# One core, convolution attention and a routed feed-forward block: constants loaded behind the first half tile of x, an inverse root in 7 operations for 9, and the weight centring in another order

## The reference, cut to what matters

```
x = x + conv_attention(ln_c(x))              # ln_c: over the 64 channels, eps 1e-6
t = tokens(x)                                # (8, 1024, 64)
t = t + ffn(ln_t(t))                         # ln_t: over the 64 channels, eps 1e-5

conv_attention(x):                           # 8 heads of 8 channels
  q, k, v = Wqkv @ x + bqkv;  q *= 8 ** -0.5
  attn = softmax(q @ k.T over n, axis=-1)    # 8 x 8 in each head
  return Wout @ (attn @ v) + bout

ffn(x):                                      # 8 experts, 2 of them for each image
  logits = mean(x over n) @ Wr + br
  w = softmax(logits); w = softmax(w * capacity_scale); top 2, softmax again
  y = sum over the two experts e of w_e * (gelu(x @ W1[e] + b1[e]) @ W2[e] + b2[e])
  return layer_norm(y + x) * gamma + beta    # eps 1e-5
```

## Time and profile before

| what | value |
|---|---|
| median of 3 runs | 119.23 us (118.2, 119.23, 119.26) |
| span of the profiled execution | 117.0 us |
| its own total | not listed; the three runs lie 1.2 to 2.3 us above the span |
| busy: TensorE, VectorE, ScalarE, GpSimd | 80%, 59%, 43%, 35% of the span |
| granted TensorE clock, mean | 0.956 |

### The profile page before, as it was taken

The page is one execution under the profiler, slowest core; times in us unless marked ns, Lnnn a source line. Parts: engine busy times, 40 slices in busy tenths (PEclk is TensorE's granted clock), DMA queues, the critical chain, the costliest instruction groups (busy, mean ns, idle before and its releaser), DMA issues.

```text
span 117.0 us, 2060 instructions
## 1 busy us (share of the span) xinstructions
PE 94.2 (80%) x626; PEld 46.6 (40%) x629; DVE 68.5 (59%) x276; ACT 50.1 (43%) x76; POOL 40.7 (35%) x93
## 2 busy tenths in 40 slices
PE   0059998989997999676599879999999998989300
PEld 0023497976763546344133223233342333234100
DVE  0299996723374188489869106835185273769850
ACT  0400504615325435407666592892983769050000
POOL 3000724900006000236801649940460550095190
PEclk9999999999999999999558999999999999999985
DMA  3999960000000000002583000560000030004124
GB/s 76 330 421 401 404 248 0 6 0 0 0 0 6 0 0 0 0 0 62 121 203 70 3 3 0 123 146 6 0 3 0 0 150 35 0 17 182 70 90 179
DMA packets 4314, 9.81 MB, mean 84 GB/s; under 512 B 592, under 2 KB 848, under 8 KB 4304
## 3 DMA queue, kind: packets, MB, share of 16 engines
q1 hardware_dynamic: 3728, 8.34, 21.6%
q10 hardware_dynamic: 576, 1.34, 3.2%
HBM read 5.49 MB, written 2.10 MB: 65 GB/s over the span
## 4 chain that ended last, share of the span: by engine, by line
PE 52%; DVE 18%; issue 8%; POOL 6%; DMA 5%; POOLq 5%; ACT 3%; ACTq 0%; DVEq 0%
PE pC L1080 10%; PE pC L886 6%; DMA cst<-consts_dram 5%; POOL XT L220 4%; PE pA L1053 4%; PE pM L956 4%; DVE UF L626 4%; PE pB L1053 4%; PE pS L827 3%; POOLq L437 3%; PE pA L837 3%; PE pM L891 2%; PE pB L949 2%; PE pC L973 2%; PE pS L891 2%
## 5 line engine op out<-in xcount | busy, mean ns | idle before, releaser
L1080 PE MATMUL pC<-H,w2g 128*64 128x512 f32 x64 | 15.8, 603 | 0.5 <-POOL w2g L452 0.5
L362 ACT ACTIVATE H<-pA,b1g 128x1024 f32<-128x1024 f32 x8 | 8.9, 1111 | 8.8 <-PE pA L1053 8.8
L535 DVE BATCH_NORM_STATS2 bst<-XT 128x6 f32<-128x64 f32 x64 | 9.4, 214 | 5.1 <-DMA XT<-x_tok_dram 5.1
L227 POOL TENSOR_TENSOR UT<-XT,rt 128x1024 f32<-128x1024 f32 x3 | 6.7, 2243 | 14.8 <-issue 10.9
L210 POOL CAST R<-r 128x16 bf16<-128x16 f32 (+1 forms) x5 | 1.0, 203 | 29.2 <-DVE r L525 29.2
L220 POOL TENSOR_TENSOR XT<-XT,T 128x512 f32<-128x512 f32 x7 | 9.2, 1334 | 4.0 <-DVE XT L788 4.0
L956 PE MATMUL pM<-cst 128*128 128x480 f32 x6 | 4.6, 904 | 7.2 <-DMA cst<-consts_dram 7.2
L753 DVE TENSOR_TENSOR c<-b2g 64x1 f32<-64x1 f32 x8 | 5.7, 716 | 5.9 <-POOL w2g L452 5.8
L966 PE MATMUL pB<-cstb 128*128 128x512 bf16 x27 | 8.8, 489 | 0.2 <-issue 0.2
L362 ACT ACTIVATE H<-pB,b1g 128x1024 f32<-128x1024 f32 x8 | 8.9, 1117 | 0.0
L419 POOL TENSOR_TENSOR LO<-UF,HI 128x1024 f16<-128x1024 f32 x4 | 8.4, 2128 | 1.2 <-ACT HI L308 1.2
(11 more groups left out here) (193 smaller groups left out, 177.1 us busy)
## 6 DMA issues: line engine op xcount, KB each, us to landing
X<-x_cha_dram SPq DMA_DIRECT2D x4, 512.0 KB, 11.3
out_dram<-XT SPq DMA_DIRECT2D x8, 256.0 KB, 2.0
XT<-x_tok_dram SPq DMA_DIRECT2D x3, 512.0 KB, 7.8
ST<-HI SPq DMA_DIRECT2D x8, 128.0 KB, 2.4
ST<-LO SPq DMA_DIRECT2D x8, 128.0 KB, 2.4
w_sb<-w_dram ACTq DMA_DIRECT2D x1, 512.0 KB, 8.1
cstb<-constb_dram ACTq DMA_DIRECT2D x1, 304.0 KB, 9.7
XT<-x_tok_dram ACTq DMA_DIRECT2D x1, 256.0 KB, 4.5
```

What stands on the lines that cost most here:

```text
L227: engine.tensor_tensor(UT[:, p, :, 1:P + 1].rearrange("p j (b c) -> p j b c", b=2), XT[:, p, :].rearrange("p (j b c) -> p j b c", b=2, c=C ...
L362: nc.scalar.activation(H[:, step % 2, b, :], h_ps[b][:, :], ACT.Gelu, bias=b1g[:, p % 2, b, k:k + 1], scale=1.0 / (S_U * S_W)).then_inc(s[ ...
L535: return nc.vector.bn_stats(bst[:, p // 2, i % (2 * G2), :], XT[:, p, g * C:(g + 1) * C])
L1080: last = mm(half(y_ps[:, cols], b), w2g[:, p % 2, b, k, :], H[:, step % 2, b, cols], start=False, stop=(k == TOP - 1))
```

## The change

It does five things. (1) ScalarE's queue waits for the first half tile of XT before it issues cst, w_sb and cstb. (2) TensorE centres the attention weights first, then W1, then experts 0 to 3 of W2, all ahead of gram(0); the third warm_up is gone and the wait for cstb moves to turn2. ScalarE copies in the same order. (3) Experts 4 to 7 of W2 are centred where the first keep_awake stood, in front of att_b1(1). (4) rsqrt has seven operations: the seed in one tensor_scalar (times -0.5, plus the magic number), and one polynomial of third degree in t = y*y*v in place of two refinements. (5) variance1 has four operations where it had five.

```diff
-RSQRT = (8 / 3) ** 2
+RSQRT = 13.314428630185905
+RS_A0, RS_A1, RS_A2, RS_A3 = -3.0727744284785232, 1.6324990948619877, 2.8033168883754556, 4.4108093219280375
...
             act.dma_start(XT[:, 0, HALF:N], x_tok[:, 0, HALF:N]).then_inc(s_xt[0], 16)
+            act.wait_ge(s_xt_first, 16)
             act.dma_start(cst[:, :], consts).then_inc(s_cst, 16)
...
-            act.wait_ge(s["w1p"], 1)
-            nc.scalar.mul(w1hl[:, :, 0, :], pC[:, :].rearrange("p (e f) -> p e f", e=E), S_W).then_inc(s["w1h"], 1)
-
             act.wait_ge(s["wcp"], 1)
...
             nc.scalar.copy(wvc[:, :], pS[:, 300:300 + C]).then_inc(s["wcv"], 1)
+            act.wait_ge(s["w1p"], 1)
+            nc.scalar.mul(w1hl[:, :, 0, :], pC[:, :].rearrange("p (e f) -> p e f", e=E), S_W).then_inc(s["w1h"], 1)
             evac_gram(0)
...
-                link(nc.vector.tensor_scalar(q, v.bitcast(U32), 1, None, ALU.logical_shift_right), between)
-                link(nc.vector.tensor_scalar(y.bitcast(U32), q, -1.0, float(0x5F3759DF), ALU.mult, ALU.add), between)
+                y, t, q = (nwt[:, i, 0:m] for i in range(3))
+                link(nc.vector.tensor_scalar(y.bitcast(U32), v.bitcast(U32), -0.5, float(0x5F3759DF), ALU.mult,
+                                             ALU.add), between)
                 link(nc.vector.tensor_tensor(t, y, y, ALU.mult), between)
                 link(nc.vector.tensor_tensor(t, t, v, ALU.mult), between)
-                link(nc.vector.scalar_tensor_tensor(out=t, in0=t, scalar=-10.0 / 3.0, in1=t, op0=ALU.add,
+                link(nc.vector.scalar_tensor_tensor(out=q, in0=t, scalar=RS_A0, in1=t, op0=ALU.add,
                                                     op1=ALU.mult), between)
-                link(nc.vector.scalar_tensor_tensor(out=y, in0=t, scalar=5.0, in1=y, op0=ALU.add, op1=ALU.mult), between)
-                link(nc.vector.scalar_tensor_tensor(out=t, in0=y, scalar=-0.5 * (3 / 8) ** 2, in1=y, op0=ALU.mult,
+                link(nc.vector.scalar_tensor_tensor(out=t, in0=q, scalar=RS_A2, in1=t, op0=ALU.add,
+                                                    op1=ALU.add), between)
+                link(nc.vector.scalar_tensor_tensor(out=t, in0=q, scalar=RS_A1, in1=t, op0=ALU.add,
                                                     op1=ALU.mult), between)
-                link(nc.vector.tensor_tensor(t, t, v, ALU.mult), between)
-                nc.vector.scalar_tensor_tensor(out=out, in0=t, scalar=1.5, in1=y, op0=ALU.add,
+                nc.vector.scalar_tensor_tensor(out=out, in0=t, scalar=RS_A3, in1=y, op0=ALU.add,
                                                op1=ALU.mult).then_inc(done, 1)
...
-                nc.vector.tensor_tensor(cmp1[:, g, 1, :], ve, vo, ALU.add)
+                nc.vector.scalar_tensor_tensor(out=cmp1[:, g, 1, :], in0=ve, scalar=C * EPS_C, in1=vo, op0=ALU.add,
+                                               op1=ALU.add)
...
             pe.wait_ge(s_cst, 16)
             warm_up(2)
 
-            pe.wait_ge(s_w12, 16)
-            for h in range(2):
-                last = mm(pC[:, h * HALF:(h + 1) * HALF], cf("cend", 0, C), w12_sb[0:C, h * HALF:(h + 1) * HALF],
-                          start=True, stop=True)
-            last.then_inc(s["w1p"], 1)
             pe.wait_ge(s_wsm, 16)
...
             last.then_inc(s["wcp"], 1)
-            warm_up(1)
+            pe.wait_ge(s_w12, 16)
+            for h in range(2):
+                last = mm(pC[:, h * HALF:(h + 1) * HALF], cf("cend", 0, C), w12_sb[0:C, h * HALF:(h + 1) * HALF],
+                          start=True, stop=True)
+            last.then_inc(s["w1p"], 1)
+            centre_w2(range(0, E // 2))
             pe.wait_ge(s["wcv"], 1)
-            pe.wait_ge(s_cstb, 16)
             gram(0)
...
             att_mt(0)
-            centre_w2(range(0, E // 2))
             conv(0)
...
             rows2(0)
-            keep_awake(5, pA[:, 0:HALF])
+            centre_w2(range(E // 2, E))
             att_b1(1)
...
             conv(3)
-            centre_w2(range(E // 2, E))
             rows2(2)
```

More of the change, by code:

```diff
@@ L112, in build_program @@
         cmp2 = sb("cmp2", [P, 2, 4, 2 * G2])
-        seed = sb("seed", [P, 2 * G2], U32)
-        nwt = sb("nwt", [P, 2, 2 * G2])
+        nwt = sb("nwt", [P, 3, 2 * G2])
         r2 = sb("r2", [P, NP, G2])
@@ L509, in link, with rsqrt @@
                 dve.wait_ge(s["dve"], count[0])
[L511 to L516 removed]
+            def rsqrt(v, m, out, done, between=None):
+                y, t, q = (nwt[:, i, 0:m] for i in range(3))
+                link(nc.vector.tensor_scalar(y.bitcast(U32), v.bitcast(U32), -0.5, float(0x5F3759DF), ALU.mult,
+                                             ALU.add), between)
                 link(nc.vector.tensor_tensor(t, y, y, ALU.mult), between)
                 link(nc.vector.tensor_tensor(t, t, v, ALU.mult), between)
[L519 removed]
+                link(nc.vector.scalar_tensor_tensor(out=q, in0=t, scalar=RS_A0, in1=t, op0=ALU.add,
                                                     op1=ALU.mult), between)
[L521 to L522 removed]
+                link(nc.vector.scalar_tensor_tensor(out=t, in0=q, scalar=RS_A2, in1=t, op0=ALU.add,
+                                                    op1=ALU.add), between)
+                link(nc.vector.scalar_tensor_tensor(out=t, in0=q, scalar=RS_A1, in1=t, op0=ALU.add,
                                                     op1=ALU.mult), between)
[L524 to L525 removed]
+                nc.vector.scalar_tensor_tensor(out=out, in0=t, scalar=RS_A3, in1=y, op0=ALU.add,
                                                op1=ALU.mult).then_inc(done, 1)
@@ L546, in variance1 @@
                 me, ve, mo, vo = (bst[:, g, :, i] for i in (1, 2, 4, 5))
-                nc.vector.tensor_tensor(cmp1[:, g, 1, :], ve, vo, ALU.add)
+                nc.vector.scalar_tensor_tensor(out=cmp1[:, g, 1, :], in0=ve, scalar=C * EPS_C, in1=vo, op0=ALU.add,
+                                               op1=ALU.add)
                 link(nc.vector.tensor_tensor(cmp1[:, g, 0, :], me, mo, ALU.subtract), between)
[L550 to L554, removed]
+                link(nc.vector.scalar_tensor_tensor(out=cmp1[:, g, 2, :], in0=cmp1[:, g, 0, :], scalar=RSQRT / 4.0,
+                                                    in1=cmp1[:, g, 0, :], op0=ALU.mult, op1=ALU.mult), between)
+                link(nc.vector.scalar_tensor_tensor(out=cmp1[:, g, 3, :], in0=cmp1[:, g, 1, :], scalar=RSQRT / C,
+                                                    in1=cmp1[:, g, 2, :], op0=ALU.mult, op1=ALU.add), between)
             def scale1(p):
@@ L614, in rstd2 @@
                     dve.wait_ge(s["pow2"], g)
-                rsqrt(cmp2[:, g, 3, :], nwt[:, 0, :], nwt[:, 1, :], seed[:, :],
-                      r2[:, 2 * g:2 * g + 2, :].rearrange("p l g -> p (l g)"), s["pow2"], between)
+                rsqrt(cmp2[:, g, 3, :], 2 * G2, r2[:, 2 * g:2 * g + 2, :].rearrange("p l g -> p (l g)"), s["pow2"], between)
             def rows2(g):
@@ L634, in _ @@
             variance1(0, more_stats)
-            rsqrt(cmp1[:, 0, 3, :], nwt[:, 0, :], nwt[:, 1, :], seed[:, :], rt1[:, 0, :], s["pow1"], more_stats)
+            rsqrt(cmp1[:, 0, 3, :], 2 * G2, rt1[:, 0, :], s["pow1"], more_stats)
             scale1(0)
@@ L640, in _ @@
             variance1(1)
-            rsqrt(cmp1[:, 1, 3, :], nwt[:, 0, :], nwt[:, 1, :], seed[:, :], rt1[:, 1, :], s["pow1"])
+            rsqrt(cmp1[:, 1, 3, :], 2 * G2, rt1[:, 1, :], s["pow1"])
             att_p1(0)
@@ L776, in rstd3 @@
                     dve.wait_ge(s["pow3"], p)
-                rsqrt(v3[:, p, :], nwt[:, 0, 0:G2], nwt[:, 1, 0:G2], seed[:, 0:G2], r3[:, p, :], s["pow3"])
+                rsqrt(v3[:, p, :], G2, r3[:, p, :], s["pow3"])
             def rows3(p):
@@ L917, in turn2 @@
                 pe.wait_ge(s["cbs"], 2)
+                pe.wait_ge(s_cstb, 16)
                 if g >= 1:
@@ L956, in warm_up, with keep_awake @@
                     mm(pM[:, 0:480], cf("ident"), cst[:, 0:480], start=True, stop=True)
[L958 to L964, removed]
+            def keep_awake(n):
+                pe.wait_ge(s["w2v"], 1)
+                bank = ps_w2
                 for _ in range(n):
```

## The result

The changed kernel takes 121.95 us (median of 4 runs, 120.98 to 124.87) against 119.25 for the kernel before: a ratio of 1.021, 95% interval 1.0133 to 1.0286. The change makes the kernel slower, by about 2% (1.3 to 2.9). Forecast were 119.1 us and no difference that can be told; the range ended at 121.0. Some executions of most kernels here take 3 to 5 us longer than the others of the same kernel (124.87 is one), and the ratios leave those out.

The account below looks back on a forecast made before the run. No one engine was taken to bound the kernel, TensorE leading with 52% of the chain. Terms +1.5 - 0.35 - 0.45 - 0.42 - 0.42 = -0.14 us gave 119.1 us against 119.23, range 117.6 to 121.0.

Parts of the forecast that it names:

- Step 1: Start of the kernel: constants issued behind the first half tile land at 8.7 us, a shift of +1.5 us.
- Rival D: Start: constants wait for all of x, SyncE's queue served first, landing at 11.1; +2.4 us, 121.5 us; chance 0.08.
- Step 2: TensorE's new order from constants to gram(0): 7.57 us against 7.58, so 0 beyond the shift.
- Step 3: First W2 half leaves its place between att_mt(0) and conv(0): -0.35 us, since conv(0) also waits for MTs.
- Step 4: Second W2 half leaves its place before rows2(2), replacing five keep_awake multiplications: 0.
- Step 5: Shorter roots and variance: -0.45 us in stage 2 group 1, -0.42 each in stage 3 tiles 1 and 3; stage 1 hidden.
- rival C: At the end VectorE's last seed starts before GpSimd's addition: -1.05 us more, 118.05 us; chance 0.06.
- Rival B: TensorE runs at its lower level (1.2 GHz) somewhere in the attention: +1.9 us, 121.0 us; chance 0.14.

Follow-up runs that it names:

- e2: The kernel before with only the wait for the first half tile added ahead of the constants: 123.48 us.
- e11: e8 with the wait ahead of the constants put back, one line different: 121.44 us, ratio to the kernel before 1.0172.
- e3: The kernel before with only the new rsqrt and variance1: 117.80 us.
- e4: The changed kernel without the wait, and with W1 and the first half of W2 centred ahead of the attention weights on TensorE: 117.26 us.
- e8: e4 with one warm-up multiplication put back between the attention weights and gram(0): 117.00 us, ratio to the kernel before 0.9855.
- e1: The changed kernel without the wait ahead of the constants: 121.98 us.
- e7: The kernel before, unchanged, run and profiled once more: 122.25 us.

## Why the prediction was wrong, point by point

**Step 1, the constants' landing: this is the step that failed.** I put it at 8.7 from a fixed part of 1.7 and "1.94 is the row nearest to it", the pace of the constants behind a half tile of their own queue while SyncE's queue moved x. That row is of a transfer issued in step with its neighbours (1.16 against 1.18 for XT tile 1). Issued at 5.09, with 1.2 MB of XT still to come in SyncE's queue, more than two tiles, it had to wait for them first: measured 6.42 us, landing 11.51, +4.33 for +1.5. The upper bound I gave, 6.02 us again, was the nearer end. Rival D came closest in time (121.5, chance 0.08), and its words "SyncE's queue served first" fit the XT tiles, not X. e2 and e11 show the price alone, about 4 us (4.2 and 3.8). The Trainium skill's fixed part plus bytes (DMA: Bandwidth & Descriptors, section Anatomy of one DMA), which gave 7.7, was further off still. The section gives these figures for transfers that GpSimd issues, and it adds nothing for what is queued ahead; for the 256 KB output tile with quiet engines an estimate by it is 2.6 us where 2.0 were measured, so the measurement decides. The same page (section Queues, rings and completion order) says that each DMA engine takes turns between the queues, packet by packet. The first 3.1 us do not show that. From 8.2 to 11.6 both queues move (0.87 and 0.45 MB), as it says.

**Step 2, order of the front: a term was missing.** I added W1 (2.05) and half of W2 (1.03) and came to 7.57 against 7.58. Measured 6.43. The chain shows their products in turn, and both together took 1.91, no longer than W1 alone in e3. That they overlap is shown (e4, e8 and the changed kernel against e3, e1 against e7). W1 lies in partitions 0 to 63 and W2 in 64 to 127; that this is why is an inference that no run tests. Worth 1.15 us, it was the largest saving of the change, and I had it at 0.

**Step 3, first W2 half: right.** -0.35 forecast, -0.33 measured between gram and conv(0).

**Step 4, second W2 half: right.** 0 forecast; the distance from 3.03 at conv(0) to the last moment rows (46.53 to 49.57) stays 3.04, and the idle time before them grew by 0.64: the work left, the wait took its place.

**Step 5, roots: right for the changed kernel.** -0.45, -0.42, -0.42 forecast; -0.44, -0.43, -0.42 in the trace. The roots of stage 1 were hidden, as said, since gram(0) waited for TensorE in every version. But they were hidden here only because gram(0) came late: in e3 they move GpSimd's scaling onto VectorE's vbs and cost 0.58 us. The prediction looked at who waits for the root, and not at what GpSimd does once it has it. The last seed kept its 1.25 us; rival C did not happen.

**The clock.** Rival B had the right thing at the wrong place. It did not fall in the attention in the profile of the changed kernel. What counts is when it rises at the start, and I treated that as the same before and after. The +0.86 at the experts is the clock again: the block of 18 took 6.74 us for 5.88, since the low stretch lay later against the routing than before. I had named no such term. The kernel before has the late rise as well, so a single pair of executions can differ by 3 us for this reason alone.

**The sum.** With the measured landing my own terms would have given +4.33 - 1.64 = +2.7; with the overlap -1.15 and the expert block +0.86 and gram's +0.18 it is the +2.6 of the spans. For the +0.18 of gram (3.78 us for 3.60) no run gives a cause.

## What to carry to other kernels

The time from issue to landing depends on what other queues already hold when the transfer is issued: moving a small transfer 4 us later made it land 4.3 us later and left the one it made way for where it was (5.1). Do not price a transfer that is issued late by its pace when it was issued early; hold back what the first engine in the chain does not need, never what it starts with. Products on the lower half of the partitions and products on the upper half, next to each other, shared their time here. A root that comes sooner lets another engine start sooner, and what that one collides with has to be looked up too. And when one kernel has executions 3 us apart, a difference of that size between two kernels is read from several runs and from the lengths of equal products, not from one pair of profiles.

## What the runs showed of the hardware that was not expected

- After an issue at 5.09 into engines busy for another queue, ScalarE's queue moved no packet for 3.1 us; with two tiles of XT and all behind them held back, it moved 61 in the same stretch.
- With both queues issuing afresh at 5 us, the engines moved 187 GB/s in place of 393.
- TensorE stayed at its lower level from 7.12 to about 19.8 in e7 though it was never idle, and in another execution of the same kernel it was past it near 11: 122.25 against 119.2 us.
- Products of 64 rows in different halves of the partitions overlapped: 1.91 us for both (e8), 1.91 for the longer alone (e3); 3.71 and 3.71 at the lower level (e1, e7).
- A VectorE instruction on 128x128 numbers took 1.81 us beside GpSimd's scaling of UT (e3), where it took 0.35 with GpSimd done (the changed kernel).
